# A decoder layer on one core: multiplications of a cleared block put into TensorE's waits in the setup

## The reference

```
x = x + attn(LN(x))                  16 heads of 16, two masked scores, softmax over 512 keys, Wo
x = x + tanh(gate) * xattn(LN(x), c) 16 heads of 64, 64 context rows, softmax, w_out, b_out
x = x + ffn(LN(x))                   a = entmax15(LN(LN(x) @ proj)) over 16 experts
                                     z = (xb @ Win1) * (a @ C1);  h = gelu(z @ Wout1.T)
                                     y = ((hb @ Win2) * (a @ C2)) @ Wout2.T
```

## Time and profile before

| | us |
|---|---|
| three runs | 1036.0, 1041.4, 1042.27 |
| their median | 1041.4 |
| span of the profiled execution, first to last instruction | 1040.1 |
| TensorE busy | 981.2 (94%) |
| VectorE busy | 768.6 (74%) |
| ScalarE busy | 616.5 (59%) |
| mean granted clock of TensorE | 0.987 of full speed |

### The profile page before, as it was taken

How to read it: one execution, slowest core, us unless ns; L and a number is a source line. 1 busy time by engine, 2 the same in 40 slices (tenths; PEclk the granted TensorE clock), 3 DMA queues, 4 the chain that set the end, 5 groups by cost and what they waited for, 6 DMA issues and landing times.

```text
span 1040.1 us, 15824 instructions
## 1 busy us (share of the span) xinstructions
PE 981.2 (94%) x5226; PEld 573.4 (55%) x5226; DVE 768.6 (74%) x1608; ACT 616.5 (59%) x857; POOL 150.0 (14%) x175
## 2 busy tenths in 40 slices
PE   5889999999989999999999999999999999999898
PEld 4434434555545645565556654565546554566676
DVE  3556756897799758986798759985898769737874
ACT  2336767555566666656665676656665675664533
POOL 2000000021012200221013100220021101211320
PEclk9889999999899999999999999999999999999999
DMA  6476885824420062111611061114411160023001
GB/s 166 130 243 215 254 257 180 267 48 122 93 72 17 16 161 64 52 33 41 183 51 30 9 183 53 31 31 125 99 51 31 30 173 22 1 82 82 1 1 42
DMA packets 77854, 97.32 MB, mean 94 GB/s; under 512 B 10435, under 2 KB 60294, under 8 KB 76774
## 3 DMA queue, kind: packets, MB, share of 16 engines
q1 hardware_dynamic: 77798, 96.63, 33.0%
HBM read 41.34 MB, written 29.36 MB: 68 GB/s over the span
## 4 chain that ended last, share of the span: by engine, by line
PE 65%; DVE 18%; ACT 6%; issue 5%; SPq 2%; DMA 2%; POOL 1%; ACTq 0%; POOLq 0%; DVEq 0%
PE y_ps L976 22%; PE x_ps L976 16%; PE pv_ps L976 8%; PE st_ps L976 7%; PE sm_ps L976 5%; DVE mx L1619 4%; PE y_ps L1139 3%; SPq L828 2%; PE y_ps L1105 2%; ACT probs L1416 2%; DVE stat L1639 1%; DVE qk_lo L1674 1%; DVE res L1691 1%; ACT qk_hi L1416 1%; DMA a_scr<-a_cat 1%
## 5 line engine op out<-in xcount | busy, mean ns | idle before, releaser
L1619 DVE TENSOR_REDUCE mx<-sm_ps 128x2 f32<-128x1024 f32 x256 | 312.1, 1219 | 116.3 <-PE sm_ps L976 116.0
L1416 ACT ACTIVATE probs<-st_ps 128x1024 f32<-128x1024 f32 x256 | 262.4, 1025 | 177.8 <-PE st_ps L976 171.9
L976 PE MATMUL pv_ps<-probs,v_all 128*32 128x512 f32 x1024 | 136.0, 608 | 0.4 <-ACT o_t L1416 0.2
L976 PE MATMUL st_ps<-q_st,k_st 52*128 52x512 f32 x512 | 124.4, 480 | 1.7 <-ACT probs L1416 1.5
L976 PE MATMUL sm_ps<-k_st,q_st 50*128 50x512 f32 x512 | 118.7, 455 | 7.1 <-DVE mx L1619 4.8
L976 PE MATMUL x_ps<-b_cat,pt 128*128 128x256 f32 x448 | 112.0, 388 | 0.0
L976 PEld LDWEIGHTS st_ps<-q_st,k_st 52*128 52x128 f32 x512 | 48.5, 184 | 97.3 <-issue 57.4
L976 PEld LDWEIGHTS x_ps<-b_cat,pt 128*128 128x128 f32 x448 | 80.0, 189 | 23.8 <-issue 13.6
L976 PEld LDWEIGHTS sm_ps<-k_st,q_st 50*128 50x128 f32 x512 | 49.2, 187 | 69.3 <-DVE mx L1619 31.7
L695 POOL TENSOR_TENSOR px<-px,cst 128x512 f32<-128x512 f32 x56 | 58.2, 1045 | 202.0 <-DVE cst L1714 202.0
L1416 ACT ACT_TABLE_LOAD x60 | 77.0, 1283 | 1.8 <-PEq L2120 0.7
(11 more groups left out here) (301 smaller groups left out, 1720.5 us busy)
## 6 DMA issues: line engine op xcount, KB each, us to landing
a_scr<-a_cat SPq DMA_DIRECT2D x16, 1024.0 KB, 5.6
a_cat<-a_scr SPq DMA_DIRECT2D x8, 2048.0 KB, 8.9
q_st<-qk_hi SPq DMA_DIRECT2D x128, 64.0 KB, 2.3
k_st<-qk_hi SPq DMA_DIRECT2D x128, 64.0 KB, 2.2
b_scr<-b_cat SPq DMA_DIRECT2D x8, 1024.0 KB, 5.1
b_cat<-b_scr SPq DMA_DIRECT2D x16, 512.0 KB, 10.8
xa<-in_x SPq DMA_DIRECT2D x9, 512.0 KB, 3.6
q_st<-qk_lo SPq DMA_DIRECT2D x64, 64.0 KB, 2.2
```

Of the source, the lines that this page charges most:

```text
L976: return nc.tensor.matmul(dst, lhs, rhs, start=start, stop=stop, **kw)
L1416: return nc.scalar.activation(dst, src, f, **kw)
L1619: nc.vector.tensor_reduce(mx[:, c % 2, :].rearrange("p (m x) -> p m x", m=2)[:, :, col], sm_ps[:], axis=AX, op=ALU.max).then_inc(sm_taken, 1)
```

## The change

A tile that is otherwise used late (`xo`) has one 128x128 block cleared by VectorE as its first instruction. TensorE multiplies this block with itself, into a bank that nobody reads, 14 times at the very beginning, twice after each `setup_w`, four times ahead of the first projections, and twice at each of 14 places `WU` in `EARLY_PE`; the first of these also waits for `qk_taken`, since they write into `pv_ps`. The rest of `EARLY_PE` keeps its order. The places follow (-2, SW, 2), (-2, SW, 6), (-1, SW, 1), (0, SW, 2), (-1, M, 19), (1, SW, 2), (1, SW, 0), (-1, M, 23), (1, SW, 4), (1, SW, 6), (1, SW, 8), (-1, M, 28), (2, SW, 0) and (2, SW, 2).

Besides, the tables of the loop are written as plain sequences (`LOOP_PE`, `LOOP_ACT`, `LOOP_DVE`, `LOOP_SP`) in the order that the tick numbers gave; ScalarE and VectorE get five more waits in a round of the loop; and for the feed forward of one sequence of the end, `Z2` writes to a part of `px` instead of `z1g`.

```diff
 EARLY_PE = (
-    (0, "SW", 0, 0), (-2, "SW", 0, 0), (-2, "SW", 1, 0), (-2, "SW", 2, 0), (-2, "SW", 3, 0), (-2, "SW", 4, 0),
+    (0, "SW", 0, 0), (-2, "SW", 0, 0), (-2, "SW", 1, 0), (-2, "SW", 2, 0), (0, "WU", 0, 0), (-2, "SW", 3, 0),
...
+WARM = 14
...
-        z2g = z1g
+        def z2_gated(g):
+            return px[:, 1].rearrange("p h s -> p (h s)")[:, 0:N] if g.reg is None and g.off == B else z1g
...
             def iteration(b):
-                for t in range(TICKS):
-                    if t % 2 == 0:
-                        score_pair(b, t)
-                    for tick, kind, i, part in PE_TASKS:
-                        if tick == t:
-                            emit(b, kind, i, part)
+                for kind, i, part in LOOP_PE:
+                    emit(b, kind, i, part)
+
+            def warm(bank, n):
+                for _ in range(n):
+                    mm(bank[:, 0:P], xo[:, 0, 0:P], xo[:, 0, 0:P], True, True)

             first = At(None, 0)
+            pe.wait_ge(warm_tile, 1)
+            warm(sm_ps[:, 1], WARM)
             pe.wait_ge(const_ready, CONSTS)
             pe.wait_ge(qk_in, 16 * 5)
             for n in range(4):
                 setup_w(n)
+                warm(sm_ps[:, 1], 2)
             setup_bias()
             for k in range(KT):
                 turn_x1(first, k)
+            warm(sm_ps[:, 1], 4)
             for j in range(4):
                 qk(first, j)
...
+                elif kind == "WU":
+                    if i == 0:
+                        pe.wait_ge(qk_taken, 4)
+                    warm(pv_ps, 2)
...
+                    if kind == "ON" and i == 0 and not is_first(g):
+                        filled(act, g + -1, "PJ", 0)
+                        filled(act, g + -1, "Z1", 1)
...
                     if kind == "Z1":
+                        if i == 0 and active(g, "G"):
+                            taken(act, g, "G", 0)
...
                     if kind == "G":
                         h, cols = half_of(g, "G", i, 2)
+                        wait(act, z2_taken, g.times(1, -1))
...
+                        if active(g, "Y") and not closing(g, kind):
+                            filled(dve, g, "Y", 1)
...
             first = At(None, 0)
+            nc.vector.memset(xo[:, 0, 0:P], 0.0).then_inc(warm_tile, 1)
             dve.wait_ge(qk_in, 16 * 5)
```

More of the change, by code:

```diff
@@ L54 @@
 S_ALL = S_MASK + 2
-PE_TASKS = (
[25 rows of a table removed]
-ACT_TASKS = (
[7 rows of a table removed]
-DVE_TASKS = (
[16 rows of a table removed]
+LOOP_PE = (
[23 rows of a table added]
+LOOP_ACT = (
[9 rows of a table added]
+LOOP_DVE = (
[12 rows of a table added]
+LOOP_SP = (
+    ("XA", 0), ("FS", 0), ("MR", 0), ("ST", 0), ("FS", 1), ("MR", 1), ("FS", 2), ("MR", 2), ("LA", 0), ("LB", 0),
+    ("RS", 0), ("FS", 3), ("MR", 3))
 LAST_PE = (
@@ L336 @@
 X_BANK = ("X1", "QK", "ZM", "O", "P", "M", "TN", "PV")
-PLAN = [u for u in PE_TASKS if u[1] not in X_BANK and u[3] == 0]
+PLAN = [u[:2] for u in LOOP_PE if u[0] not in X_BANK and u[2] == 0]
 LAST = B - 1
@@ L499, in build_kernel @@
         small = sem("small")
+        warm_tile = sem("warm_tile")
         tanh_done = sem("tanh_done")
@@ L571, in plan @@
         def plan(g):
-            return [u for u in PLAN if active(g, u[1])]
+            return [u for u in PLAN if active(g, u[0])]
         def in_tail(g, kind, i):
@@ L593, in order @@
                 return SU_EARLY + early.index((kind, i))
-            n = [u[1:3] for u in plan(g)].index((kind, i))
+            n = plan(g).index((kind, i))
             if g.reg is None:
@@ L598, in order @@
             return SETUP_UNITS + before + len(PLAN) * (g.off - 2) + n
-        early = [(u[0], u[2]) if u[1] == "SW" else u[1:3] for u in EARLY_PE if u[1] not in X_BANK and u[3] == 0]
+        early = [(u[0], u[2]) if u[1] == "SW" else u[1:3] for u in EARLY_PE if u[1] not in X_BANK + ("WU",) and u[3] == 0]
         def setup_no(p, n):
@@ L939, in iteration @@
             def iteration(b, store_=True, project=True, row=None):
-                if project:
-                    load_xa(b + 2, row)
-                for c in range(CH):
-                    if c == 3:
+                for kind, c in LOOP_SP:
+                    if kind == "XA" and project:
+                        load_xa(b + 2, row)
+                    if kind == "LA":
                         load_a(b)
+                    if kind == "LB":
                         load_b(b)
+                    if kind == "RS":
                         load_res(b)
-                    if project:
+                    if kind == "FS" and project:
                         fill_stack(b + 1, c)
-                    if c < 2:
+                    if kind == "MR" and c < 2:
                         fill_maxrow(b, c + 2)
-                    elif project:
+                    elif kind == "MR" and project:
                         fill_maxrow(b + 1, c - 2)
-                    if c == 0 and store_:
+                    if kind == "ST" and store_:
                         store(b + -3)
@@ L1232, in result @@
                 for t in (2 * n, 2 * n + 1):
-                    last = mm(y[:, D * (t % 2):D * (t % 2) + D], z2g[:, P * t:P * t + P], wout2_t[:], True, True)
+                    last = mm(y[:, D * (t % 2):D * (t % 2) + D], z2_gated(g)[:, P * t:P * t + P], wout2_t[:], True, True)
                 last.then_inc(y_full, 1)
@@ L1566, in iteration @@
             def iteration(b):
-                for t in range(TICKS):
-                    if t % 2 == 0:
-                        softmax_exp(b, t)
-                    for tick, kind, i in ACT_TASKS:
-                        if tick == t:
-                            emit(b, kind, i)
+                for kind, i in LOOP_ACT:
+                    emit(b, kind, i)
             def w_hi_part(n):
@@ L1925, in task @@
                         taken(dve, g + -1, "G", 2 * h + 1)
-                        nc.vector.scalar_tensor_tensor(out=z2g[:, cols], in0=z2_bank(g, kind, h), scalar=zbias[:, 1:2],
+                        nc.vector.scalar_tensor_tensor(out=z2_gated(g)[:, cols], in0=z2_bank(g, kind, h), scalar=zbias[:, 1:2],
                                                        in1=g2s[:, cols], op0=ALU.add, op1=ALU.mult).then_inc(z2_taken, 1)
@@ L1956, in iteration @@
             def iteration(b):
-                for t in range(TICKS):
-                    for tick, kind, i in DVE_TASKS:
-                        if tick == t:
-                            emit(b, kind, i)
+                for kind, i in LOOP_DVE:
+                    emit(b, kind, i)
             def small_parts():
```

## The result

The changed kernel takes 1044.16 us (median of 17 runs, 1040.32 to 1049.73) against 1040.78 us for the kernel before in 17 runs beside them: a ratio of 1.0041, 95% interval [1.0025, 1.0057]. That is slower by 0.4%, where 1034.5 us and a gain were forecast, and 1.2 us above the forecast's range (1029 to 1043). The profiled execution has a span of 1041.4 us.

The account below looks back on a forecast made before the run. TensorE, busy for 981.2 of 1040.1 us, was taken as the bound. A -3.1, B -1.4 and C -2.6 gave -7.1 us; with 1.3 for the median over the span, 1034.3, rounded to 1034.5 us, range 1029 to 1043.

Parts of the forecast that it names:

- A: The start, to 27 us: added products raise TensorE's clock early; 4.8 us won at best, 3.1 counted.
- 5.6 us can pass by the first store of A: SP's idle time from 46.66 to 48.98 us lets a start gain of up to 5.6 us through.
- B: 28 to 38 us: the 24 products of 256 columns speed up if the clock holds; -1.4 us (-2.0 to +1.2).
- C: 47 to 80 us: 4.6 us won if the clock holds, less 2.0 for five places; -2.6 us (-4.6 to +3.8).
- the one lapse counted on: Between 11 and 14 us the clock falls back once, taking 1.7 us from the start's gain.
- the transposes' 0.7: At the start, the tokens' transposes halve; 0.7 of about 1.0 us remains as gain.
- The price of a product: One added multiplication costs 0.43 us at the lower clock, 0.25 at the higher; a place of two 0.5 us.
- The waits and the other tile: Five added waits per iteration and another tile for the last gated product: all waits met on arrival, cost 0.
- The first: Rival: the clock holds everywhere with no lapse; -10.4 us, 1031 us; chance 0.17.
- The third: Rival: cleared blocks do not raise the clock, or not for long; +4.4 us, 1046 us; chance 0.08.
- The second: Rival: the clock does not hold through C; about -1.5 us in all, 1040 us; chance 0.2.
- The fourth: Rival: SP's stack fills and stores decide 48 to 65 us, losing the start's gain; 1039 us; chance 0.1.

Follow-up runs that it names:

- e1: The changed kernel with the load of the second sequence's tokens issued ahead of the 12 row fills: 1039.6 us, ratio 0.9984 to the kernel before.
- e2: The kernel before with the load of the second sequence's tokens issued ahead of the 12 row fills: 1040.9 us, ratio 1.0004.
- e14: The changed kernel with the second and fourth sequences' token loads both issued earlier: 1036.3 us, ratio 0.9956 to the kernel before.
- e15: The changed kernel with only the products of the start, none at the 14 places, and both token loads earlier: 1035.7 us, ratio 0.9936.
- e17: The kernel before, no added products, with both token loads issued earlier: 1038.5 us, ratio 0.9983.
- e4: The changed kernel without the 26 products of the start, the 14 places kept: 1039.6 us, ratio 0.9989 to the kernel before.
- e5: The changed kernel without any of the products of the cleared block: 1041.2 us, ratio 0.9983 to the kernel before.
- e13: The changed kernel with only the fourth sequence's token load moved into the middle of its stack fill: 1041.7 us, ratio 1.0001 to the kernel before.
- e6: The changed kernel with the 13 small loads issued by ScalarE instead of SP: 1042.0 us, ratio 0.9999 to the kernel before.
- e9: The changed kernel with SP's queue reordered: second tokens between the row fills, seven small loads behind the first stack fill: 1048.0 us, ratio 1.0071.
- e12: The changed kernel without the products at the last five of the 14 places: 1044.2 us, ratio 1.0031 to the kernel before.
- e16: The changed kernel with the 12 row fills issued by GpSimd instead of SP: 1040.2 us, ratio 0.9982 to the kernel before.
- e3: The changed kernel without the products at the 14 places, those of the start kept: 1042.3 us, ratio 1.0003 to the kernel before.
- e7: The kernel before, without products, with the 13 small loads issued by ScalarE instead of SP: 1042.3 us, ratio 0.9999.
- e8: The changed kernel with only the products of the start and the 13 small loads issued by ScalarE: 1039.8 us, ratio 0.9964.

## Why the prediction was wrong

**The failing step is the last sentence of A,** "so 5.6 us can pass by the first store of A". I had seen that SP issues until 25.2 us, read its load at 24.85 us only as what stands ahead of the stack fills, and went on to the store. The load has a reader of its own: VectorE, in order, ahead of low parts that TensorE needs. TensorE's lead went there, between 27 and 30.5 us: -3.7 became +0.9 (e1, e2). As to SP alone the sentence was right: with the tokens there, the first store of A goes out at 44.02 us (e14) instead of 48.98. In the profile of the change the account stands at +0.6 us at 40 us, where A and B should have left -4.5, at +0.9 at 100, where C should have left -7.1, and at +3.1 behind the fourth sequence's tokens.

**A's size was right.** Forecast -3.1, best -4.8; measured -3.7 by 27 us in the change, with the one lapse counted on (the projections' first row is late behind the transposes at 14 to 17 us). Of its terms, the small products won 1.2 (12.60 to 13.99 against 12.53 to 15.15 us) where 1.3 stood, and the projections 2.5 (17.32 to 23.11 against 18.53 to 26.82 us) where 2.8 stood; the transposes' 0.7 did not come, as the lapse lay on them. e15, whose profile has no lapse, is 5.2 us ahead at 27 us. Where nothing takes it back, the start is worth 0.47% or 4.9 us in the medians (e15 against e17; by their two intervals, good to some 0.3%).

**The price of a product was right:** 28 records from 1.05 to 7.39 us are 0.45 us per product of two records at the lower clock (0.43 taken), and the place at 40.60 us holds TensorE for 0.54 us (0.5 taken). The clock had been expected to rise before all 14 were done; in this profile it rose only at their end (7.3 us), which cost nothing: the first turn starts at 7.18 instead of 7.11 us.

**B, -1.4, was right in size and gone in the change; that the places bring it is not shown.** From 27 to 40 us e14, where the tokens are there, goes from -3.8 to -5.4, that is -1.6, with the clock at 1.00 through the transposes; e15, without the places, has 0.57 there and wins 0.1. But in e2, without any product, the 24 products take 2.9 us too (32.79 to 35.70 us), and e4, with the places, is at 0.54 in 30 to 35 us. In the change the standstill had brought the lower clock back before B began. The rule of the Trainium skill that I had weighed ("TensorE: Matmul & The Clock Gate", "Part 4: PE-mode transpose", that transposes don't count as busy as products do) agrees with e14 against e15, but not with the five profiles whose clock stays at 1.00 through the same burst of transposes without the places. What decides it in one execution and not in the next is open.

**C, -2.6, was mis-sized.** The rows fell, 3.48 to 1.98 us as forecast, 2.08 to 1.36 (1.13 forecast) and 2.67 to 1.76 (half forecast). But the places cost +0.9 us from 46 to 65 us, where I had five as covered, and one stay at the lower clock remained. Net from 46 to 100 us: -0.2 in the change, -0.6 in e14, -2.0 in e4, whose clock held throughout; and the kernel before, with only its loads moved, already gains 1.5 there with a shorter stay (e17).

**The waits and the other tile, 0,** were right (e5), as was "the loop is unchanged" (+1.8 at 320 and +1.7 at 950 us).

**A loss that no step held** is the fourth sequence's tokens at 193 us: +2.5 us in the profile, and 0.40% in the medians (e13 against the change). It is A's mistake once more: I had looked for late loads only as far as the places reach.

**The rivals.** The first is refuted: the clock fell in 25 to 30, 65 to 70 and 195 to 200 us. The third is refuted: cleared blocks do raise the clock. The second was half right: C's clock fell again, less long. The Trainium skill's section "HAM oscillation — how this bites in real kernels" of the same page, that waits between bursts bring the lower clock back, agrees with 0.50 behind the 4.35 us and with 0.66 behind the 1.74 us, but not each time: in e6 a wait of 1.80 us at the same place leaves the clock at 1.00. It has no say on which wait. The fourth came nearest: the start's gain is lost later because of SP. I had put it at 48 to 65 us and argued that SP waits there. True, but the place was 20 us earlier, and there SP waits for nothing.

**What stays open.** Why the places together with the start meet the late load at 193 us more than either alone. In the profiles of the change, e6, e9, e12, e13 and e16 one pair of fill DMAs ahead of that load occupies SP for 2.4 to 2.7 us; in those of the kernel before, e1, e3 and e4 for 1.23. VectorE then waits 2.4 to 3.0 us in the former (0.3 in e13, where the load stands earlier), 0.95 to 1.5 in the latter. What makes that pair slow was not found.

## What to carry to other kernels

Before counting a gain on one engine, list for every in-order engine the next load that it will reach, when the issuing queue comes to that load, and whether anything the change speeds up moves that time; a load that lands just in time is a wall for any lead. Here a gain of some 5 us at the start was worth nothing (e3) until two loads were moved ahead of DMAs that nothing needed sooner (e15). And a wall met with the clock up can cost twice: behind the standstill of 4.35 us the work ran at the lower clock until 38 us. Last, a pair of profiles is thin evidence on the clock: two executions of the same program can differ by more than the change does.

## What the runs showed of the hardware

- Products of zeros raise TensorE's clock: 28 cleared records from 1.05 us on, 0.23 us each, with the higher clock behind them; four from 40.60 us on hold TensorE for 0.54 us, 0.14 each.
- The granted clock is recorded as 1.00 where the products show the lower level: at 20 to 25 us before. So the mean clock, 0.987 in both, leaves the cold start out, and can't be compared between these kernels.
- What TensorE did before does not settle by itself where the clock falls: 1.74 us of idle time ahead of 193.76 us were followed by 0.66 (195 to 200 us of the change), 1.80 us at the same place in e6 by 1.00; and of e2 and e17, the same program up to 178 us, one has 1.00 and the other 0.61 in 30 to 35 us.
- With loads issued early by ScalarE, one issued by SP landed later: the bias at 9.2, 8.5 and 9.0 us (e6, e7, e8) instead of 7.1. Row fills issued by GpSimd took it 0.5 us each, on SP 0.7, and nothing waited for them (e16).
